# Attention stage of a two-layer block on one core: ScalarE copies a finished head's output before it raises the scores of the unit three further on, where it did so after

## The reference

```
q = (text_hidden @ Wq).reshape(B, T_text, N_HEADS, HEAD_DIM).transpose(0, 2, 1, 3)
scores = jnp.einsum('bhtd,bhsd->bhts', q, k) / scale
scores = jnp.where(mask, scores, -jnp.inf)
attn = jax.nn.softmax(scores, axis=-1)
out = jnp.einsum('bhts,bhsd->bhtd', attn, v)
out = out.transpose(0, 2, 1, 3).reshape(B, T_text, N_HEADS * HEAD_DIM)
return out @ Wo
```

## Time and profile before

| | |
|---|---|
| Median of three executions | 668.95 us |
| The profiled execution | 668.65 us |
| Its span, first to last instruction | 666.9 us |
| PE busy | 612.8 us, 92% of the span |
| DVE, ACT, POOL busy | 480.9, 411.7, 307.2 us |
| Attention loop, by the rows | about 342 to 556 us of the span |

### The profile page before, as it was taken

The page is one execution under the profiler, slowest core; times in us unless marked ns, Lnnn a source line. Parts: engine busy times, 40 slices in busy tenths (PEclk is TensorE's granted clock), DMA queues, the critical chain, the costliest instruction groups (busy, mean ns, idle before and its releaser), DMA issues.

```text
span 666.9 us, 11178 instructions
## 1 busy us (share of the span) xinstructions
PE 612.8 (92%) x3736; PEld 512.5 (77%) x3736; DVE 480.9 (72%) x1046; ACT 411.7 (62%) x845; POOL 307.2 (46%) x306
## 2 busy tenths in 40 slices
PE   6656779999999999999999999999999999969995
PEld 2355544666777888888888999999999988759984
DVE  5999999999975665446557666667678865754455
ACT  4886666775336546445567777877867677624441
POOL 1456630122344334445456655765546788240314
PEclk9689989999999999999999999999999999989999
DMA  6677865667563263544339422242111212344644
GB/s 201 184 254 271 292 215 165 194 204 221 161 191 118 93 199 124 157 157 135 105 99 351 152 80 81 83 151 84 32 32 46 75 67 70 120 132 150 210 151 126
DMA packets 58151, 98.90 MB, mean 148 GB/s; under 512 B 7016, under 2 KB 26992, under 8 KB 58096
## 3 DMA queue, kind: packets, MB, share of 16 engines
q1 hardware_dynamic: 56560, 94.00, 44.4%
q0 software_dynamic: 1536, 4.20, 2.0%
HBM read 78.51 MB, written 19.66 MB: 147 GB/s over the span
## 4 chain that ended last, share of the span: by engine, by line
PE 65%; DVE 16%; issue 7%; ACT 7%; POOL 2%; DMA 1%; another core or an unknown queue 1%; DVEq 0%; SPq 0%; POOLq 0%; ACTq 0%
PE bank L101 18%; PE bank L103 17%; PE bank L102 17%; DVE state L1571 6%; PE bank L911 3%; PE bank L999 2%; ACT bank L1112 2%; POOL w_lo L2202 1%; PE bank L963 1%; DVE u_sb L1496 1%; PE bank L692 1%; PE bank L579 1%; ACT probs L1368 1%; DVE x_tok L1610 1%
## 5 line engine op out<-in xcount | busy, mean ns | idle before, releaser
L2202 POOL TENSOR_TENSOR w_lo<-w_raw,w_hi 128x512 fp32r<-128x512 f32 (+1 forms) x78 | 120.6, 1548 | 153.8 <-ACT w_hi L1076 80.4
L101 PE MATMUL bank<-xt_hi,w_hi 128*128 128x512 f32 x256 | 104.4, 408 | 1.6 <-POOL w_lo L2202 1.0
L103 PE MATMUL bank<-xt_hi,w_lo 128*128 128x512 f32 x256 | 101.1, 395 | 0.0
L102 PE MATMUL bank<-xt_lo,w_hi 128*128 128x512 f32 x256 | 100.8, 394 | 0.0
L1076 ACT ACTIVATE w_hi<-w_raw 128x512 fp32r<-128x512 f32 (+1 forms) x78 | 56.6, 726 | 47.6 <-PE bank L103 45.5
L1368 ACT ACTIVATE probs<-scores,row_min 128x256 f32<-128x256 f32 x128 | 63.8, 501 | 15.8 <-DVE row_min L2009 15.8
L2315 POOL TENSOR_TENSOR probs<-probs,row_scale 128x512 f32<-128x512 f32 x64 | 66.6, 1041 | 5.0
L2009 DVE CUSTOM_DVE_ANT_0 scores<-bank,mask_bias 128x256 f32<-128x256 f32 x128 | 48.8, 420 | 17.3 <-PE bank L103 17.3
L1076 ACT ACTIVATE probs_t_hi<-bank 128x512 fp32r<-128x512 f32 x64 | 38.2, 598 | 32.7 <-PE bank L911 32.3
L101 PEld LDWEIGHTS bank<-xt_hi,w_hi 128*128 128x128 f32 x256 | 48.2, 188 | 12.3 <-POOL w_lo L2202 3.6
L103 PEld LDWEIGHTS bank<-xt_hi,w_lo 128*128 128x128 f32 x256 | 48.1, 188 | 11.7
(11 more groups left out here) (263 smaller groups left out, 1820.2 us busy)
## 6 DMA issues: line engine op xcount, KB each, us to landing
w_raw<-in_ffn_w SPq DMA_DIRECT2D x46, 384.0 KB, 3.5
b_rows<-bc_scratch SPq DMA_DIRECT2D x32, 256.0 KB, 5.0
c_rows<-bc_scratch SPq DMA_DIRECT2D x32, 256.0 KB, 4.0
w_raw<-fold_scratch SPq DMA_DIRECT2D x32, 256.0 KB, 2.8
experts<-in_ffn_w SPq DMA_DIRECT2D x16, 384.0 KB, 4.3
route_bc<-route_scratch SPq DMA_DIRECT2D x31, 192.0 KB, 3.4
slots_scratch<-nothing SPq DMA_DIRECT2D x2, 2944.0 KB, 13.3
slots_in<-slots_scratch SPq DMA_DIRECT2D x22, 256.0 KB, 2.8
```

The costliest lines, as they stand in the source:

```text
L101: e.matmul(out, w_hi, m_hi, start=first, stop=False)
L102: e.matmul(out, w_hi, m_lo, start=False, stop=False)
L103: return e.matmul(out, w_lo, m_hi, start=False, stop=last)
L2202: e.tensor_tensor(lo[:, 0:n], w_raw[(p - WHOLE) % RAW][:, 0:n], hi[:, 0:n].bitcast(F32), ALU.subtract).then_inc(sem("w_lo"), 1)
```

## The change

The two lines that call `round_head(i - 3)` in ACT's loop are moved up, ahead of `soften(i)` and of the two early calls of `round_projected`:

```diff
@@ -1414,12 +1414,12 @@
             for i in range(HEAD_UNITS + 4):
                 if 0 <= i - 2 < HEAD_UNITS:
                     round_probs(i - 2)
+                if 0 <= i - 3 < HEAD_UNITS:
+                    round_head(i - 3)
                 if i < HEAD_UNITS:
                     soften(i)
                 if i < 2:
                     round_projected(i, 1 - i)
-                if 0 <= i - 3 < HEAD_UNITS:
-                    round_head(i - 3)
```

## The result

The changed kernel takes 672.45 us (median of 6, 670.86 to 673.93) against 668.85 us for the kernel before (median of 6, 668.39 to 670.51, with the three shown earlier). The ratio is 1.0043, its 95% interval 1.0027 to 1.0060: slower by 0.43%, 2.9 us by the ratio and 3.6 by the medians. The forecast was 672.3. The profiled execution took 670.86 us, its span is 669.1 (before 668.65 and 666.9).

What follows compares the result with a forecast made beforehand. PE, busy 92% of the span, was taken to set the time. Terms 3.4 + 0.6 - 0.4 - 0.2 = 3.4 us on 668.65 gave 672.05; with the median 0.3 above, 672.3 us was predicted, range 669.2 to 675.0.

Steps and rivals of the forecast that it cites:

- E: End of the last matmul of a head product on PE, from which the prediction measures its chain.
- the 18 steady ones: Attention-loop pairs whose next product into bank 7 started at E + 2.30 or 2.31: 0.19 us each, 3.4 us slower.
- 60 and 62: Late loop pairs where PE has no `project` left and already waits: E + 2.17 becomes E + 2.47, 0.30 us each.
- 4, 14, 16: Pairs whose exponential waited for DVE's late mask, the copy behind it on the path: gains of 0.4, 0.10, 0.24 us.
- 36, 40, 56: Pairs where DVE reaches the reciprocal late because of its own routing work: no change claimed.
- Step 1: ACT's copy of bank 7 can't start before PE has filled it: start at E + 0.04, held up by 0.22 us.
- Step 2 to 4: ACT and DVE after the copy: exponential E + 0.53, reciprocal E + 1.65, rest of the head from E + 1.73 to 2.42.
- Step 5: PE restarts 0.05 behind the rest, at E + 2.47 against 2.30: 0.17 us, plus 0.02 for a longer first matmul.
- The cover: 2.7 us on the probabilities' transposes and 0.46 us idle on ACT hide the exponential's 0.71 us delay from PE.
- No difference: Rival: the copy-to-PE chain is a little shorter than read, so the price nears its lower bound; 668.4 to 670.8 us, chance 0.17.
- Far more: Rival: the exponential's delay reaches PE through DVE's queue; 681.7 us, or 675.3 with half of it, chance 0.10.
- Faster: Rival: DVE's rest waited for the copy wherever PE stood, so moving it gains; 667.2 us, chance 0.04.

Runs made afterwards that it cites:

- the second pair of traces: Kernel before and changed kernel, both unchanged, traced again on other chips than the first: loops 210.67 and 214.10 us.
- the last experiment: Kernel before with ACT's head copy moved ahead of the exponential only at i = 4, 14 and 16: 667.98 us against 668.74, one execution each.

## Why the prediction was right, step by step

The largest check is the time of each pair of iterations, from one E to the next, changed against before:

| pairs | forecast, us | by the traces |
|---|---|---|
| the 18 steady ones | 18 x 0.19 = 3.42 | 3.42 (0.16 to 0.25 each) |
| 60 and 62 | 0.60 | 0.56 |
| 4, 14, 16 | -0.41 - 0.10 - 0.24 | -0.42 - 0.12 - 0.27 |
| 12 | +0.10 | +0.06 |
| 36, 40, 56 | 0 | 0.01 + 0.07 + 0.04 |
| the rest | 0 | -0.02 |
| sum | 3.4 | 3.33 |

- *Step 1, the copy held by E.* Forecast E + 0.04, found E + 0.03 or 0.04 in 29 of the 30 pairs. The other is i = 12, at 0.23, where the copy of bank 6 ahead of it was itself late.
- *Step 2 to 4.* At i = 20: exponential E + 0.53, reciprocal E + 1.64 (forecast 1.65), rest from E + 1.72 (1.73).
- *Step 5.* The rest is 0.67 long when it follows the reciprocal directly and not 0.69, as the row of i = 36 had already shown, so PE restarts at E + 2.45 where I said 2.47. I had overlooked that row's own duration. In exchange the restart costs 0.04 and not 0.02: the pair takes 0.15 + 0.04 = 0.19 longer. Two errors of 0.02 cancel, and that they do is luck.
- *The cover.* Probabilities, weights and the odd units cost PE nothing, and the experiment with the reciprocal behind the rest shows it: there the exponential is as late as in the changed kernel, and 17 of the 18 steady pairs are at 2.30. In the changed kernel only 54 and 58 paid 0.05 to 0.06 more than the steady price: their reciprocal began at E + 1.70. Routing was not the cause, since DVE had done with it and stood idle for the exponential for 0.53 and 0.40 us; the exponential itself was on time, at E + 0.53 and 0.54. Why the reciprocal came later behind it stays open.
- *The end of the kernel.* It follows the loop: from the loop's end to the end of the span are 107.08 us before and 107.29 after. The span of the profiled execution grew by only 2.2 us because the part ahead of the loop, which the change does not touch, took 1.34 us less in it (349.12 and 347.78 us to E at i = 4); in the second pair of traces it took 350.89 and 350.05.
- *The figure of the Trainium skill, "ScalarE: Activation LUTs", section "What ACT_TABLE_LOAD costs".* The issue step behind the new copy is 0.50 us in the row of i = 20 and 0.49 at others. The 0.52 estimated from its figures for an ACTIVATE was too long by the trace, and the sum by it, 4.0, too large for the loop's 3.33.
- *Wrong in it:* that PE's waits in the list would rise to over 20 times and by 3 to 4 us. They did not move (6.1 and 3.6 us before, 6.1 and 3.7 after). I took a list that shows only gaps between drawn instructions for one that shows stands. The gap from E to the next product, which I also named, was the right thing to look at. The chances, too, were added up loosely: by their own split "same" comes to 0.26 and "faster" to 0.02, where 0.25 and 0.03 are stated.
- *Rivals.* No difference: it needed a gap of 2.30, and it is 2.45. Far more: it needed a second releaser on PE, and there is none. Faster: the gain where the exponential is late exists, 0.81 us at 4, 14 and 16, but 36, 40 and 56 gained nothing, and the 18 steady pairs and 60 and 62 were not free.

## What to carry to other kernels

What this kernel shows is that an instruction gains by moving up only where its consumer can use it earlier. Here the copy went ahead of the exponential, but on the next engine the consumer of the copy stood behind the consumer of the exponential, so the move lengthened the chain; with both engines' orders changed together the same move gains 5 us, and in the three pairs where the exponential was late it gains 0.8 us alone. And a chain that is hidden with 0.14 us to spare should be priced by its length against the engine's own work, since the busy share of a full engine and its list of waits do not show a stand of 0.15 us.

## What the runs showed of the hardware

The same kernel takes 668.85 us on the first chip, 668.74 in its one execution beside the last experiment, and 659.18 and 659.67 on two others. Its loop is the same to 0.03 us in the two traces that there are, one from the first chip and one from the last named. The windows from 590 to 605 us, the kernel before on the first chip and on a later one (us, busy PE, PEld, DVE, ACT, POOL, granted clock, DMA share, GB/s):

```profile
590.00:605.00 15.00, 9.23 (x55) 8.38 (x54) 4.52 (x9) 4.03 (x8) 3.46 (x4) 0.77 0.31 102
```

```profile
590.00:605.00 15.00, 14.51 (x102) 13.02 (x101) 8.97 (x25) 6.47 (x14) 4.80 (x5) 1.00 0.56 178
```

On the first chip PE is busy for 9.23 of these 15 us; on the other it is busy for 14.51, with the clock granted in full, 2.4 GHz. The mean of 0.77 on the first is made of both levels, as its windows of 2 us show:

```profile
592.00:594.00 2.00, 0.45 (x5) 0.21 (x3) 0.00 (x0) 0.60 (x1) 1.54 (x2) 1.00 0.35 127
594.00:596.00 2.00, 1.03 (x4) 0.58 (x4) 0.00 (x0) 0.00 (x0) 0.38 (x1) 1.00 0.64 195
596.00:598.00 2.00, 0.00 (x0) 0.00 (x0) 0.89 (x2) 0.82 (x2) 0.00 (x0) 0.54 0.22 76
600.00:602.00 2.00, 2.00 (x11) 2.00 (x10) 0.69 (x1) 0.60 (x1) 0.00 (x0) 0.50 0.84 256
604.00:606.00 2.00, 2.00 (x19) 2.00 (x18) 0.10 (x1) 0.81 (x2) 0.00 (x0) 1.00 0.21 62
```

PE does little from 592 us on and nothing from 596 to 598, and there the clock falls to its lower level, 1.2 GHz; from 600 to 602 PE is busy throughout at 0.50, and from 604 on it has the upper level again. In this trace the chain of waits spends 5.31 us, from 590.70 us, on a transfer or queue that it can't name. Which one it is, and why the other chip doesn't have it, no run here settles.

Behind the loop the first chip takes 9.64 us more (107.08 against 97.44). About 7.3 of them come between 565 and 603 us, by two DVE instructions that start at 565.13 and 603.34 on the first chip and at 566.83 and 597.72 on the other; about 2.1 more come behind 654 us. The whole is nearly three times what the change costs, so totals from different chips can't be held against each other here.
